# Counting edge kinds from unsorted edges beside the attention's tables, and a second scatter split between two stages

## What is computed

```python
h = relu(layernorm(x)); q, k, v = h @ Wq + bq, h @ Wk + bk, h @ Wv + bv     # 4 heads of 32
a = (q[src] * k[dst]).sum(-1) / sqrt(32)
agg = segment_sum(v[src] * segment_softmax(a, dst), dst)                     # then gate, norm, PReLU
x = x + ...
h = relu(layernorm(x)); xw[r] = h @ weight[r]                                # 8 relations
src_all, dst_all = concat(src, dst), concat(dst, src)                        # both directions
seg = edge_type_all * n + dst_all
agg = segment_sum(xw[edge_type_all, src_all], seg)
deg = segment_sum(ones, seg)                                                 # 8 x n counts
x = x + sum_r(agg[r] * where(deg > 0, 1 / max(deg, 1), 0)) + h @ self_weight
```

## Time and profile before

| | us |
|---|---|
| median of 3 runs | 16595.82 |
| fastest, slowest of the 3 | 16594.39, 16609.32 |
| the profiled execution, its own time | 16622.33 |
| its span, first to last instruction | 16620.6 |
| GpSimd (POOL) busy | 11030.3 (66%) |
| TensorE (PE) busy | 10337.5 (62%) |
| VectorE (DVE) busy | 8708.3 (52%) |
| ScalarE (ACT) busy | 2590.7 (16%) |
| mean granted clock of TensorE, share of full speed | 0.614 |

### The profile page before, as it was taken

How to read it: one execution, slowest core, us unless ns; L and a number is a source line. 1 busy time by engine, 2 the same in 40 slices (tenths; PEclk the granted TensorE clock), 3 DMA queues, 4 the chain that set the end, 5 groups by cost and what they waited for, 6 DMA issues and landing times. The chain is left out here.

```text
span 16620.6 us, 205783 instructions
## 1 busy us (share of the span) xinstructions
PE 10337.5 (62%) x59883; PEld 8534.7 (51%) x60300; DVE 8708.3 (52%) x26923; ACT 2590.7 (16%) x6666; POOL 11030.3 (66%) x11472
## 2 busy tenths in 40 slices
PE   6733347777677777555555455554577777877777
PEld 2200036666666665334444444443566664666666
DVE  9900037777777778775555555555333332333331
ACT  0011123333333332121111111111000001100000
POOL 4777777777777772027777777776677771477773
PEclk9955568777888777675555555555555555555555
DMA  2011122222222222232222322223222222222222
GB/s 77 11 55 52 50 65 63 62 63 62 64 63 64 63 62 58 94 107 58 57 58 56 55 62 61 61 62 54 64 62 61 62 62 46 75 58 58 58 57 40
DMA packets 689254, 1005.85 MB, mean 61 GB/s; under 512 B 233758, under 2 KB 487660, under 8 KB 688172
## 3 DMA queue, kind: packets, MB, share of 16 engines
q0 software_dynamic: 392896, 680.65, 17.6%
q1 hardware_dynamic: 295276, 312.01, 6.2%
HBM read 812.97 MB, written 178.86 MB: 60 GB/s over the span
## 5 line engine op out<-in xcount | busy, mean ns | idle before, releaser
L642 POOL DMA_INDIRECT far_rel_dst<-table_xw,recs_rel_dst x1664 | 1600.2, 962 | 1410.0 <-DMA recs_rel_dst<-rec_dst 903.2
L1488 DVE TENSOR_TENSOR acc<-banks,acc 128x145 f32 (+1 forms) x3328 | 1011.4, 304 | 2712.6 <-PE banks L1472 2350.3
L642 POOL DMA_INDIRECT far_sum_dst<-table_h,recs_sum_dst x1664 | 1578.9, 949 | 1025.2 <-DMA recs_sum_dst<-rec_dst 518.4
L642 POOL DMA_INDIRECT far_sum_src<-table_h,recs_sum_src x1664 | 1578.0, 948 | 651.0 <-issue 426.9
L642 POOL DMA_INDIRECT far_att<-table_qv,recs_att x1664 | 1621.6, 975 | 572.2 <-issue 502.5
L541 POOL DMA_INDIRECT rec_dst<-stage_dst_sort,row_dst_sort x1563 | 1515.9, 970 | 680.3 <-issue 476.0
L642 POOL DMA_INDIRECT far_rel_src<-table_xw,recs_rel_src x1664 | 1588.6, 955 | 533.5 <-issue 506.8
L1364 DVE TENSOR_TENSOR acc<-banks,acc 128x128 f32 x3328 | 969.6, 291 | 1703.0 <-PE banks L1319 1339.1
L749 POOL DMA_INDIRECT rec_src<-moved_att,row_src x1563 | 1527.3, 977 | 476.5 <-issue 470.4
L1471 PE MATMUL banks<-far_sum_src,hot_sum_src 128*128 128x128 f32 x3328 | 1285.1, 490 | 746.2 <-issue 574.3
L1471 PE MATMUL banks<-far_sum_dst,hot_sum_dst 128*128 128x128 f32 x3328 | 1285.1, 490 | 641.0 <-issue 579.9
(11 more groups left out here) (292 smaller groups left out, 22416.5 us busy)
## 6 DMA issues: line engine op xcount, KB each, us to landing
table_xw<-xw_rel_tables SPq DMA_DIRECT2D x98, 512.0 KB, 2.6
far_att<-table_qv,recs_att POOLq DMA_INDIRECT x1664
far_rel_dst<-table_xw,recs_rel_dst POOLq DMA_INDIRECT x1664
far_rel_src<-table_xw,recs_rel_src POOLq DMA_INDIRECT x1664
far_sum_src<-table_h,recs_sum_src POOLq DMA_INDIRECT x1664
far_sum_dst<-table_h,recs_sum_dst POOLq DMA_INDIRECT x1664
rec_dst<-stage_dst_sort,row_dst_sort POOLq DMA_INDIRECT x1563
rec_src<-moved_att,row_src POOLq DMA_INDIRECT x1563
```

The costliest lines, as they stand in the source:

```text
L642: e.indirect_dma_start(out=self.far[:, g % RING, t, :], out_offset=None, in_=table, in_offset=bass.IndirectOffsetOnAxis(ap=index, axis=0)) ...
L1488: e.tensor_tensor(acc[:, bass.ds(at[t], 1), :], bank(g0, t).unsqueeze(1), acc[:, bass.ds(at[t], 1), :], ALU.add).then_inc(k.s_sum, 1)
```

## The change

- In `sort_edges` each column of 128 unsorted edges gets on VectorE a one-hot of the src node's place in its window (`at_place`, 128 wide, bf16) and one of (window, pair of kinds), 98 x 4 = 392 wide, with the value 1 for the first kind of the pair and 4,096 for the second (`at_pair`, two operations in one instruction, both with a value per partition). TensorE multiplies the two, so that PSUM collects the counts of all windows at once. 16 columns (KC) belong to each of the 98 windows of tables, in four sets of four with three buffers; `tally` splits each window's sum into the two kinds by a mask and a shift and adds them to `k.inverse`. Five conversions over all 1,563 columns and two small ones precede the windows. VectorE does `kinds_of` and the `tally` of the window before ahead of its copy of q and v; TensorE does the 16 matmuls behind the window's own.
- `count_edges` is gone. Its last addition (dst counts) is the first new operation in front of the reciprocal in `attention_to_relation`.
- The scatter of "src" records: MOVE = 12 a block in all 104 blocks of the attention (three a group), 1,248 in all. The other 315 (LATER) are done by GpSimd in `attention_to_relation`, where SP loads them in one transfer of 315 x 21 numbers per partition ahead of x.
- Buffers are laid over each other to find the space (`qv`, `kept`, `begin`, `seen`, `w_skip`, `w_agg`).

```diff
-MOVES = -(-ET // BT)
+
+MOVE = 12
+MOVES = BLOCKS
+LATER = ET - MOVES * MOVE
+assert LATER > 0
+
+KC = -(-ET // W)
+KG = -(-KC // 4)
+K2 = R // 2
+FIELD = 4096
...
+def fours(w):
+
+    end = min((w + 1) * KC, ET)
+    return [range(c, min(c + 4, end)) for c in range(w * KC, end, 4)]
...
+            follow()
+            then(e.tensor_scalar(tmp_i[:, :], typ_i[:, :], 1, None, ALU.arith_shift_right))
+            follow()
+            then(e.scalar_tensor_tensor(out=key[:, :], in0=win["src"][:, :], scalar=float(K2), in1=tmp_i[:, :], op0=ALU.mult, op1=ALU.add))
+            follow()
+            then(e.tensor_scalar(key[:, :], key[:, :], float(W * K2 // 2), None, ALU.subtract))
+            then(e.tensor_scalar(tmp_i[:, :], typ_i[:, :], 1, None, ALU.bitwise_and))
+            follow()
+            then(e.tensor_scalar(worth[:, :], tmp_i[:, :], float(FIELD - 1), 1.0, ALU.mult, ALU.add))
+            then(e.tensor_copy(pair[:, :], pair_i[:, :]))
+            then(e.tensor_copy(place[:, :], k.col[:, :]))
+            follow()
+
+        def kinds_of(e, w):
+            for j, four in enumerate(fours(w)):
+                n, b = KG * w + j, (KG * w + j) % 3
+                if n >= 3:
+                    e.wait_ge(s_kinds, n - 2)
+                for t, c in enumerate(four):
+                    e.tensor_scalar(at_place[:, b, t, :], place[:, :], loc["src"][:, c:c + 1], None, ALU.is_equal)
+                    i = e.tensor_scalar(at_pair[:, b, t, :], pair[:, :], key[:, c:c + 1], worth[:, c:c + 1], ALU.is_equal, ALU.mult)
+                i.then_inc(s_kind, 1)
+
+        def tally(e, w):
+
+            n = 5 * w
+            e.wait_ge(s_kinds, KG * w + len(fours(w)))
+            if w:
+                e.wait_ge(s_tally, n)
+            e.tensor_copy(counted[:, :], k.psum[6 + w % 2][:, 0:W * K2]).then_inc(s_tally, 1)
+            e.wait_ge(s_tally, n + 1)
+            e.tensor_scalar(first_kind[:, :], counted[:, :], FIELD - 1, None, ALU.bitwise_and).then_inc(s_tally, 1)
+            e.tensor_scalar(second_kind[:, :], counted[:, :], 12, None, ALU.arith_shift_right).then_inc(s_tally, 1)
+            for i, one in enumerate((first_kind, second_kind)):
+                mine = k.inverse[:, 0:W, :].rearrange("p w (a i) -> p (w a) i", i=2)[:, :, i]
+                e.wait_ge(s_tally, n + 2 + i)
+                e.tensor_tensor(mine, mine, one[:, :], ALU.add).then_inc(s_tally, 1)
...
+                kinds_of(e, w)
+                if w:
+                    tally(e, w - 1)
                 s = w % 4
                 e.wait_ge(s_mm, w + 1)
                 if w >= 4:
                     e.wait_ge(k.s_store[s], 16 * (w // 4))
                 e.tensor_copy(qv[:, s, :], k.psum[2 + s][:, 0:2 * F]).then_inc(s_qv, 1)
+            tally(e, W - 1)
...
+                for j, four in enumerate(fours(w)):
+                    n = KG * w + j
+                    e.wait_ge(s_kind, n + 1)
+                    if w >= 2 and not j:
+                        e.wait_ge(s_tally, 5 * (w - 2) + 1)
+                    for t, c in enumerate(four):
+                        i = e.matmul(k.psum[6 + w % 2][:, 0:W * K2], at_place[:, n % 3, t, :], at_pair[:, n % 3, t, :],
+                                     start=(c == w * KC), stop=(c == min((w + 1) * KC, ET) - 1))
+                    i.then_inc(s_kinds, 1)
...
-                if c < MOVES:
-                    b, n = c % NREC, columns(c)
-                    if c >= NREC:
-                        e.wait_ge(s_placed[b], placed(c - NREC))
-                    e.dma_start(moved[:, b, 0:n, :], k.raw_src[:, c * BT:c * BT + n, :]).then_inc(s_moved[b], 16)
+                b = c % NREC
+                if c >= NREC:
+                    e.wait_ge(s_placed[b], placed(c - NREC))
+                e.dma_start(moved[:, b, :, :], k.raw_src[:, c * MOVE:(c + 1) * MOVE, :]).then_inc(s_moved[b], 16)
...
-                c, first = g // RG, g % RG * GT
-                if c >= MOVES:
-                    continue
+                c, first = g // RG, g % RG * (MOVE // RG)
                 b = c % NREC
                 if first == 0:
                     e.wait_ge(s_moved[b], 16 * (c // NREC + 1))
-                for i in range(first, min(first + GT, columns(c))):
-                    t = c * BT + i
+                for i in range(first, first + MOVE // RG):
+                    t = c * MOVE + i
...
-def count_edges(k):
...
+            chained(e.tensor_tensor(cnt, cnt, k.sums[:, 0:W, HD:], ALU.add))
+            follow(e)
...
+        def gpsimd(e):
+            e.wait_ge(s_moved, 16)
+            for i in range(LATER):
+                t = ET - LATER + i
+                e.indirect_dma_start(out=flat_src, out_offset=bass.IndirectOffsetOnAxis(ap=k.row_src[:, t:t + 1], axis=0),
+                                     in_=moved[:, i, :], in_offset=None).then_inc(s_placed, 16)
+            e.wait_ge(s_placed, 16 * LATER)
+
         def sync(e):
+            e.dma_start(moved[:, :, :], k.raw_src[:, ET - LATER:ET, :]).then_inc(s_moved, 16)
```

83 lines of the change are left out of this document (28 added, 55 removed).

## The result

| | before | changed |
|---|---|---|
| median, us | 16599.2 (4 runs, 16594.4 to 16609.3) | 15912.9 (4 runs, 15912.4 to 15919.0) |
| profiled execution, its span | 16622.3, 16620.6 | 15913.3, 15911.1 |
| mean granted clock | 0.614 | 0.642 |

The ratio is 0.9587, 95% interval 0.957 to 0.9603: 686 us less, where 718 were forecast (15878). On another chip the two kernels took 16623.9 and 15927.6 us, ratio 0.9584 (0.9568 to 0.96). On three more chips the kernel before itself took 20164 to 20354 us. The changed kernel as it stands was not run on these; two versions of it with small edits that still do all the work were, and they were no faster than before (20172.2 against 20164.2, 20362.7 against 20354.5). The experiments come to that.

A forecast was written before the change was run, and what follows sets the result against it. GpSimd was taken to pace sort and attention and to idle in counting pass and tables. Terms -478 - 342 + 22 + 80 = -718 us from the median 16595.8 gave 15878 us, range 15790 to 16100.

The forecast's parts named there:

- Attention: Attention stage: GpSimd paces 2,912 steps at 1.281 us, plus a 27 us tail, 6004 instead of 6483: -478 us.
- Rival B: Attention: a group of gathers stays at 9.64 us, +280, 16158 us in all; chance 0.07.
- Counting pass: Separate pass between attention and relations' tables: removed whole, nothing hides it, -342 us.
- Tables: Relations' tables: load ahead of x 13 us, addition 1, scatters beside the stores 8: +22 us, the 315 scatters hidden.
- D: Relations' tables: scatters at 1.86 us each outlast the stage, +82, 15960 us in all; chance 0.10.
- Sort: Sort with the new counting: scatters 0.06 us slower each (65 us), start 15 us later: +80 us, ends +10 and +320.
- Window: One window of the sort: the chain of matmuls, column set and tally takes 12.1 us at 1.2 GHz.
- Like marking 390: Sort, wide comparison on VectorE: priced at 0.248 us, as a mark of 390 values.
- C: Sort: GpSimd shut out for each run of columns, 5.4 us a window, +545 instead of +80, 16343 us; chance 0.06.
- A: Sort: wide operation runs one element a cycle, 0.5 us, +290 instead of +80, 16088 us in all; chance 0.14.
- E: Sort: columns built so slowly that windows set the pace; at 1.3 us a column 16871 us, slower than before; chance 0.03.
- the sign: Whole kernel: faster by over 0.2% at 0.96, within 0.2% at 0.01, slower at 0.03.

The follow-up runs named there:

- The split alone: Kernel before with 12 scatters a block in the attention and the last 315 beside the relations' tables, counting pass kept: 0.9918 of before, on two chips.
- the other order: Changed kernel with 32 columns of later records, parameters and first skip rows loaded before x and the other 283 columns: 15907.8 us, 0.9568 of before.

## Why the prediction was right, and where it was off

**What bounds each stage.** Right on chips like the first: attention and sort at GpSimd's rate, the counting pass and the tables without it.

**Attention, 35 of its 478 us short.** The step "2,912 steps x 1.281" failed in its second factor: 1.293. The gathers kept their length (976 ns before, 977 now), the scatters went from 977 to 1,002 ns, and 1,248 x 0.025 are 31 of the 35 us. VectorE's busy share in this stage rose from 2830 / 4006 = 71% to 2997 / 3764 = 80%; that a scatter therefore meets a VectorE operation more often is my reading, and against it stands that the gathers beside the same VectorE kept theirs. The split alone did not run on a chip like the first. On the others a scatter of the attention took 971 ns with 16 a block, and 976 to 977 with 12 a block, with the new counting as without it: there the counting has no part in it. Rival B fell: the clock rose to 0.91, and GpSimd waited for the mix of a group for 0.3 us in all.

**Counting pass.** -342 forecast and measured, with nothing left of it elsewhere.

**Tables, 9 us less than forecast.** The load ahead of x: "24.9 x 3.4 / 6.4 = 13 us later" was 35.5 - 27.0 = 8.5 us (wait from the stage's start to the first operation, 6108.9 to 6144.5; before 6825.3 to 6852.3). The scatters beside the stores: 8 taken; 13.4 - 8.5 - 1.0 for the addition leaves 4, and the run without them said 2 to 5. The scatters themselves: (342.8 + 101.1) / 315 = 1.41 us each, 1.46 forecast, and done 56 us before the next gather, so D fell.

**Sort, 11 us less.** Start: GpSimd waited 31.7 us for ScalarE instead of 16.1, +15.6, forecast +15, though 3.7 of it came 88 us later. Slower scatters: (1089.0 + 329.6) / 1083 = 1.310 us against (1036.8 + 330.0) / 1083 = 1.262, from the group of scatters in that part of the sort (both shown above): +0.048 where 0.06 was taken, 52 us against 65. In the trace 455 of the 1,083 scatters last over 0.985 us, and what they exceed 0.958 us by is 51 us in all; that VectorE's operations do this fits the run with one narrow comparison in four, but TensorE's and the stores' part was not separated.

Window: copies of q and v at 864.72 and 876.71 us, 12.0, forecast 12.1; 98 of them fit beside the scatters. The chain is the forecast one, term by term: up to the fourth set of columns 7.75 us (forecast 6.46 + 1.3), the set 1.96 (1.7), the tally and the copy 2.28 (2.6). What was wrong in it is the price of the comparisons: 0.25 and 0.18 us, overlapping by 0.05, make 0.38 a column, measured 0.47. "Like marking 390" took a mark with a number in the instruction as the pattern for a comparison with two numbers per partition. The 0.33 us for a matmul held, but by luck: the earlier trace rows give it as a duration at the higher clock (0.98 in that stretch), and here it is the distance of two starts at a mean clock of 0.61, with a duration of 0.53. The errors in the window nearly cancel, which is luck too. It didn't matter, as the run with five buffers shows: GpSimd had the longer way.

C, the long lock, fell by the same 0.048 us: GpSimd got in between the operations. In the run of 12 columns from 865.06 to 870.64 us its scatters began at 865.46, 866.72, 868.10 and 869.47 us. So far these rows agree with the rule of the Trainium skill (SBUF — State Buffer, SBUF: two separate sides), a lock for one instruction, on the side on which the forecast had put it. A fell: the wide operation takes 0.31 us from start to start, not 0.5.

**E and the sign.** On chips like the first the sign was never in doubt. On the other chips the nearest kernel, that with 335 scatters beside the tables, came out "within 0.2%" (1.0005), to which 0.01 had been given. In the sort E's mechanism came true there: the windows set it, with 2.1 us from one wide comparison to the next (in the kernel with bf16 scalars, 2385.01 and 2387.09 us) where E needed 1.1. That its +535 us is near C's 545 is chance, for GpSimd was not shut out. The cause under it stood in no rival: no row of the profile of before hinted that engines stand still beside GpSimd, for on that chip they don't. So the forecast is right for chips like the first; that its kernel was timed on one of them was luck.

## To carry to other kernels

Work moved beside an engine that is the bound costs what that engine is slowed by (here 0.05 us a scatter in the sort), not what the work itself takes; price it per instruction of the bound engine, then look at whether the cover is long enough, and fill the cover up to its end (335 scatters instead of 315). Small loads that others wait for go ahead of big ones on the same queue. A gain that rests on overlap with GpSimd's indirect transfers should be timed on more than one chip: here it was 686 us on one kind and, by the stages and the nearest kernels, none on the other.

## What was not expected of the hardware

- On three of the chips TensorE and VectorE got through less than a fifth of their instructions while GpSimd issued scatters beside the marks of the sort, and through all of them when it did not; a program of 16,600 us took 20,164 to 20,354 us.
- A queue can stand on an issue: behind the loads of 3.4 and 6.4 MB the issue of the next small load took SP 27.7 us (L1273 above), and all parameters were issued after it. In the other order the issue of a parameter took 0.4 to 0.6 us. Why it stands, the traces don't tell.
- Comparisons of 392 and 128 bf16 values with per-partition scalars followed each other at about 0.3 and 0.16 us, whether the scalars were f32 or bf16, though each lasted 372 and 243 ns by itself: the end of one lies some 0.08 us behind the start of the next.
